# First layer of a two-layer attention kernel: y turned by VectorE and moved through DRAM, statistics moved to ScalarE, each block move one load

## The chip, the cores and the metric

One core of one Trainium2 chip runs the whole kernel in one launch. The metric is the device time of an execution in microseconds, from the first to the last instruction with what lies around it.

## The reference

Two attention layers run over x of shape (32, 256, 256): 32 samples of 256 tokens and 256 features, 16 heads of 16. All is float32.

```python
# layer 0
xn  = layer_norm(x, norm_w, norm_b)
q, k = (xn @ q_w + q_b), (xn @ k_w + k_b)                 # 16 heads
att = softmax(einsum('bnhl,bmhl->bnmh', q, k) + mask, axis=2)
v   = (xn @ v_w + v_b) * src_mask[:, :, None]
y   = einsum('bnmh,bmhl->bnhl', att, v)
h   = layer_norm(y, sb_norm_w, sb_norm_b) * (1 + scale) + shift   # scale, shift from the condition
x   = x + silu(h) @ out_w + out_b
# layer 1: k = softmax over tokens (masked), q = softmax over features, y = q (k^T v), then the same ending
```

## The kernel before, in words

**Stages.** The first layer's attention is a loop of 32 turns `t`, one new sample per turn, in which every engine runs a hand-written order; the tail after it finishes the last samples. Then comes the second layer, as rounds `second(t)`, one sample a round. Semaphores tie the engines together; nothing is scheduled by a tool, so the order of the work is the order of the calls in each engine's block.

**One turn of the first layer.** TensorE computes q, k and v of sample t (`qk`, `vals`), the scores of sample t-1 for their row maxima (`rowmax`, 8 units), the scores again with the maxima subtracted for the exponentials (`scores`, 8 units), and P·V of sample t-4 (`values`, four groups of heads, into the PSUM bank psY, a 17th row giving the sum for the softmax). VectorE reduces the maxima (L1158), ScalarE takes the exponentials (L741) and adds the q and k biases (L764), GpSimd splits q and k into a high and a low part (`split`, L518 and L521), and SyncE issues all DMAs: `parts(t, 0)` and `parts(t, 1)` move six pieces of 256 KB into the tiles Qs and Ks (L326, L328), with a zero block (L323) and mask rows (L320); `c_in` writes the maxima (L346).

**The way of y before.** ScalarE copies psY to the tile yT (`yturn`, L778), TensorE turns it by 128x128 transposes back into psY (L1746), VectorE divides by the sums (`divide`, L1191 and L1193) and takes mean and variance of the rows (`ystats`, L1199 and L1201), GpSimd normalizes (`ynorm`, L503 to L511) into Yn, `ystore` writes Yn to DRAM (L350) and the second half of the kernel loads it by blocks (`yload`, L372, four DMAs).

**The way of x before.** VectorE takes the statistics of x (`stats`, L1090 and L1092), GpSimd normalizes into xs (`xnorm`, L472 to L488), `nstore` writes it to DRAM (L332), `nblocks` loads it back as blocks of 32 rows (L342, four DMAs of 64 KB), and VectorE turns the blocks (`xturn`, L1172). xB, the tile they are loaded into, has one buffer. In the second layer `fstore` and `fload` (L381, L390) do the same for its y. A store before is one DMA with 2 KB in a row, and a load is four DMAs of 512 B runs:

```python
sp.dma_start(xnd[n], xs[:, :, :, :, :].rearrange("p a i k c -> p (a i k c)")).then_inc(s_nd, 16)
...
by_block = xnd[n].rearrange("(b s) (a e) -> a s b e", s=32, a=4)
for q in range(4):
    sp.dma_start(tile[32 * q:32 * q + 32, :, :], by_block[q]).then_inc(s_nb, 16)
```

## Time and profile before

| what | value |
|---|---|
| three runs, median (lowest to highest) | 868.77 us (867.59 to 869.85) |
| the profiled execution | 869.6 us |
| its span, first to last instruction | 867.8 us |
| TensorE busy in the span | 832.3 us (96%) |
| VectorE busy | 773.2 us (89%) |
| ScalarE busy | 679.0 us (78%) |
| GpSimd busy | 679.9 us (78%) |
| mean granted TensorE clock | 0.994 of full speed |
| bytes moved by DMA | 143.69 MB in 129847 packets |

The busy times are of one profiled execution, and are averages over stages that differ: the ramp up to about 80 us, some 26 like turns of the first layer up to about 480 us, its tail up to about 540 us, and the rounds of the second layer. The profile also gives, for any stretch of time, how many packets the core's 16 DMA engines moved and their mean busy share.

### The profile page before, as it was taken

The page shows a single profiled execution, that of the slowest core. Times are in us where ns is not written, and L with a number is a line of the kernel's source. Part 1 is how long each engine was busy: PE and PEld are TensorE (multiplying, and loading weights), DVE is VectorE, ACT ScalarE, POOL GpSimd, SP SyncE. Part 2 cuts the span into 40 slices and gives each one's busy share as a digit, 9 for nine tenths or more (in the row PEclk, how much of TensorE's full clock was granted, in tenths as well). Part 3 has the DMA queues.
Part 4 walks back from the last instruction along what each step waited for, and adds up shares of the span by engine and source line. Part 5 has one row for each costly group of instructions (what it writes and reads, how often), then busy time and mean ns, then how long its engine had stood idle before and what let it go on. Part 6 is the DMA issues. An engine that isn't in the chain of part 4 may idle for free.

```text
span 867.8 us, 23658 instructions
## 1 busy us (share of the span) xinstructions
PE 832.3 (96%) x8092; PEld 686.9 (79%) x8092; DVE 773.2 (89%) x1590; ACT 679.0 (78%) x1208; POOL 679.9 (78%) x1165
## 2 busy tenths in 40 slices
PE   4999999999999999999999988999999999999996
PEld 4777777777777777777777656899999999999996
DVE  6689999999998999999998967899999999999976
ACT  2247777777777777777778796899999999999975
POOL 3375878878888888888786337899999999999965
PEclk9899999999999999999999999999999999999999
DMA  8854665565656565655654424345454444444311
GB/s 258 263 175 165 198 219 187 207 209 191 220 183 212 179 222 181 221 196 196 219 178 164 142 64 107 96 126 144 152 149 143 136 142 140 138 150 141 116 31 62
DMA packets 129847, 143.69 MB, mean 166 GB/s; under 512 B 13312, under 2 KB 85984, under 8 KB 129600
## 3 DMA queue, kind: packets, MB, share of 16 engines
q1 hardware_dynamic: 129728, 142.19, 50.5%
q8 instruction: 65, 1.06, 0.5%
q14 instruction: 54, 0.44, 0.2%
HBM read 49.50 MB, written 38.11 MB: 101 GB/s over the span
## 4 chain that ended last, share of the span: by engine, by line
PE 77%; DVE 13%; issue 6%; POOL 1%; ACT 1%; SPq 1%; DMA 0%; DVEq 0%; ACTq 0%; POOLq 0%
PE psY L1721 12%; PE psX L1600 11%; PE psT L1600 10%; PE psM L1600 10%; DVE sb_cm L1158 6%; PE psT L1700 5%; PE psY L1600 5%; PE psT L1679 4%; PE psT L1883 3%; PE psY L1836 3%; PE psT L1611 3%; PE psM L1700 3%; PE psY L1746 2%; DVE sb_xF L1172 2%; PE psM L1679 2%
## 5 line engine op out<-in xcount | busy, mean ns | idle before, releaser
L1158 DVE TENSOR_REDUCE sb_cm<-psT 128x4 f32<-128x1024 f32 x168 | 202.8, 1213 | 20.5 <-PE psT L1700 20.3
L741 ACT ACTIVATE sb_P<-psT 128x1024 f32<-128x1024 f32 x176 | 177.8, 1026 | 42.6 <-PE psY L1721 23.5
L1721 PE MATMUL psY<-sb_P,sb_Vp 128*17 128x256 f32 x2048 | 129.4, 381 | 1.9 <-DVE sb_yr L1193 1.2
L1158 DVE TENSOR_REDUCE sb_cm<-psM 128x4 f32<-128x1024 f32 x88 | 106.7, 1213 | 11.5 <-PE psM L1700 11.5
L741 ACT ACTIVATE sb_P<-psM 128x1024 f32<-128x1024 f32 x80 | 82.0, 1025 | 21.6 <-PE psY L1721 11.7
L1600 PE MATMUL psX<-sb_xT,sb_W0h 128*128 128x256 f32 x488 | 93.6, 294 | 0.0
L1721 PEld LDWEIGHTS psY<-sb_P,sb_Vp 128*17 128x17 f32 x2048 | 50.3, 97 | 46.8 <-DVE sb_yr L1193 1.9
L521 POOL TENSOR_TENSOR sb_qp<-sb_qp 128x512 fp32r<-128x512 f32 x64 | 82.3, 1285 | 5.3
L1700 PE MATMUL psT<-sb_Ks,sb_Qs 64*128 64x256 f32 x672 | 76.6, 310 | 2.6 <-DVE sb_cm L1158 2.5
L1679 PE MATMUL psT<-sb_Qs,sb_Ks 64*128 64x256 f32 x704 | 75.5, 298 | 1.6 <-ACT sb_P L741 1.4
L1600 PEld LDWEIGHTS psX<-sb_xT,sb_W0h 128*128 128x128 f32 x488 | 71.4, 192 | 4.6 <-ACT sb_qp L764 0.2
L1700 PEld LDWEIGHTS psT<-sb_Ks,sb_Qs 64*128 64x128 f32 x672 | 50.1, 185 | 27.9 <-issue 12.6
L1679 PEld LDWEIGHTS psT<-sb_Qs,sb_Ks 64*128 64x128 f32 x704 | 53.2, 185 | 17.3 <-issue 10.2
L764 ACT ACTIVATE sb_qp<-psX,sb_bq 128x256 f32<-128x256 f32 x122 | 51.1, 472 | 11.0 <-PE psX L1600 11.0
L1600 PE MATMUL psX<-sb_xT,sb_W0l 128*128 128x256 f32 x244 | 48.9, 282 | 0.0
L595 POOL TENSOR_TENSOR sb_rs<-sb_ve,sb_ph 128x2 f32<-128x2 f32 x63 | 44.6, 708 | 5.3
L1746 PE MATMUL psY<-sb_ident,sb_yT 128*128 128x128 f32 x256 | 40.3, 280 | 5.7 <-DVE sb_yr L1193 1.3
L503 POOL TENSOR_SCALAR sb_ve<-sb_mv 128x2 f32<-128x2 f32 x32 | 7.3, 228 | 43.9 <-DVE sb_mv L1201 43.7
L1700 PE MATMUL psM<-sb_Ks,sb_Qs 64*128 64x256 f32 x352 | 40.7, 309 | 0.6 <-ACT sb_P L741 0.5
L1600 PE MATMUL psM<-sb_Woh,sb_v 128*128 128x256 f32 x256 | 41.0, 282 | 0.0
L611 POOL TENSOR_TENSOR sb_v<-sb_v,sb_rb 128x512 f32<-128x512 f32 x32 | 41.0, 1282 | 0.0
L518 POOL TENSOR_SCALAR sb_qp<-sb_qp 128x512 fp32r<-128x512 f32 x64 | 39.7, 621 | 0.7 <-ACT sb_qp L764 0.7
(215 smaller groups left out, 2553.4 us busy)
## 6 DMA issues: line engine op xcount, KB each, us to landing
sb_Qs<-sb_qp SPq DMA_DIRECT2D x96, 256.0 KB
sb_Ks<-sb_qp SPq DMA_DIRECT2D x96, 256.0 KB
sb_xt<-in_x SPq DMA_DIRECT2D x32, 256.0 KB, 3.4
y_normed<-sb_Yn SPq DMA_DIRECT2D x32, 256.0 KB, 2.7
sb_u<-y_normed SPq DMA_DIRECT2D x128, 64.0 KB, 2.6
out<-sb_v SPq DMA_DIRECT2D x31, 256.0 KB, 2.4
x_biased<-sb_xo SPq DMA_DIRECT2D x28, 256.0 KB, 2.3
sb_u<-x_biased SPq DMA_DIRECT2D x28, 256.0 KB, 3.3
```

The costliest lines, as they stand in the source:

```text
L518: g.tensor_scalar(qp[w][:, 0, :, :].bitcast(F32R), qp[w][:, 1, :, :], 1.0, 0.0, ALU.mult, ALU.add)\
L521: g.tensor_tensor(qp[w][:, 1, :, :].bitcast(F32R), qp[w][:, 1, :, :], qp[w][:, 0, :, :], ALU.subtract)\
L595: g.tensor_tensor(rs[:, k], ve[:, k], ph[:, :], ALU.pow).then_inc(e_rs[l], 1)
L611: g.tensor_tensor(x1[n % 7], x1[n % 7], ob1, ALU.add).then_inc(e_xo, 1)
L741: a.activation(P[G % 4][:, :], pairs[place["S", n, g][0]][:, :], ACT.Exp).then_inc(s_ex, 1)
L764: ins = a.activation(qp[w][:, 1, o, :], home("qk"[w], n)[:, T * o:T * o + T], ACT.Identity, bias=bq[:, 2 * w + o:2 * w + o + 1])
L1158: v.tensor_reduce(cm[n % 2][:, 4 * j:4 * j + 4], scores, AX.X, ALU.max, negate=True).then_inc(s_mx, 1)
L1600: ins = pe.matmul(dst, part(lhs[a], d, o), part(rhs[b], d, r), start=(m == 0), stop=(m == 5))
L1679: ins = pe.matmul(pair[:, c:c + 256], Ks[n % RING][p:p + 64, g, 128 * m:128 * m + 128].bitcast(F32R), Qs[n % RING][p:p + 64, g, :].bitcast ...
L1700: ins = pe.matmul(pair[:, c:c + 256], Qs[n % RING][p:p + 64, j, 128 * k:128 * k + 128].bitcast(F32R), Ks[n % RING][p:p + 64, j, :].bitcast ...
L1721: ins = pe.matmul(psY[32 * j:32 * j + 17, y0:y0 + T], Vp[n % RING][:, m, 4 * gr + j, :], Pj[:, c0:c0 + 256], start=(m == 0), stop=(m == 1))
L1746: ins = pe.transpose(psY[:, 128 * q:128 * q + 128], yT[n % 2][:, q, 128 * k:128 * k + 128], ident[:, :])
```

## The change

What it does, part by part:

- **y.** TensorE no longer turns y of samples 0 to 27 (`TAIL = B - 4`), and ScalarE no longer copies it. VectorE turns psY in 32x32 blocks straight into the tile yG (`yblock`), takes the reciprocals (`yroot`), GpSimd multiplies (`share`) into yq, SyncE writes yq to DRAM (`qstore`, runs of 256 B) and loads it back with tokens on the partitions (`qload`), and a turn later VectorE takes the statistics (`ylanded`) and GpSimd normalizes (`ynorm`). Samples 28 to 31 go the old way.
- **x.** From sample 10 on (`SUMMED`) ScalarE makes the sums (`xsum`, `xsquares`, four passes with an accumulator), and GpSimd turns them into mean and variance.
- **masks.** `vmask` moves from GpSimd to ScalarE.
- **block moves.** `nstore`, `ystore` and `fstore` now write 512 B runs in the order the load wants, and `nblocks`, `yload` and `fload` are one DMA each with 2 KB runs.
- **order.** `xturn` on VectorE moves from the middle to the end of a turn; SyncE's `nstore` and `nblocks`, `xstore` and `xload` move ahead of `parts`; the maxima's turn `cturn` moves behind the seventh unit of scores. The heads of a psY group are 4 apart now, and the host packs q's and k's weights accordingly.

```diff
             def nstore(n):
-                sp.dma_start(xnd[n], xs[:, :, :, :, :].rearrange("p a i k c -> p (a i k c)")).then_inc(s_nd, 16)
+                sp.dma_start(xnd[n].rearrange("(s a) (b e) -> b (s a) e", a=4, b=4),
+                             xs[:, :, :, :, :].rearrange("p a i k c -> p a (i k c)")).then_inc(s_nd, 16)
             def nblocks(n):
                 sp.wait_ge(s_nd, 16 * (n - BY_BLOCK + 1))
                 if n > BY_BLOCK:
                     sp.wait_ge(s_xf, n - BY_BLOCK)
-                for q in range(4):
-                    sp.dma_start(tile[32 * q:32 * q + 32, :, :], by_block[q]).then_inc(s_nb, 16)
+                sp.dma_start(xB[:, :, :].rearrange("p k t -> p (k t)"),
+                             xnd[n].rearrange("(s a) e -> a s e", a=4)).then_inc(s_nb, 16)
...
+            def qstore(n):
+                sp.wait_ge(s_yq, 2 * n + 2)
+                sp.dma_start(qd[n].rearrange("r (k j e) -> j (r k) e", k=2, j=4), yq.rearrange("p (x e) -> p x e", e=64))\
+                    .then_inc(s_qd, 16)
+            def qload(n):
+                sp.wait_ge(s_qd, 16 * (n + 1))
+                if n >= 2:
+                    sp.wait_ge(s_y, n - 1)
+                sp.dma_start(yrs[n % 2].rearrange("p k d -> p (k d)"), qd[n].rearrange("(s b) e -> b s e", b=4))\
+                    .then_inc(s_yl[n % 2], 16)
...
+                if 0 <= t - 5 < TAIL:
+                    qstore(t - 5)
+                if t >= BY_BLOCK and ok(t + 2):
+                    nstore(t + 2)
+                if 0 <= t - 5 < TAIL:
+                    qload(t - 5)
+                if 0 <= t - 6 < TAIL:
+                    ystore(t - 6)
...
+                if t >= BY_BLOCK and ok(t + 2):
+                    nblocks(t + 2)
+                    xstore(t + 2)
+                if t >= BY_BLOCK and ok(t + 4):
+                    xload(t + 4)
...
+            def share(n, half):
+                g.wait_ge(s_yi, 2 * n + half + 1)
+                if half == 0 and n >= 1:
+                    g.wait_ge(s_qd, 16 * n)
+                root = ri[:, half, :].rearrange("p (g b a) -> p g b a", g=2, a=1).to_broadcast([128, 2, 8, DH])
+                g.tensor_tensor(yq.rearrange("p (b g d) -> p g b d", b=8, g=4)[:, 2 * half:2 * half + 2],
+                                yG[half][:, :, :, 0:DH], root, ALU.mult).then_inc(s_yq, 1)
...
+            def xsum(n):
+                for k in range(2):
+                    a.activation(xn[:, k, :], xt[n % 2][:, k, :], ACT.Identity, accum_out=sx[:, 0, k:k + 1])\
+                        .then_inc(s_sx, 1)
+            def xsquares(n):
+                for k in range(2):
+                    a.activation(xn[:, k, :], xt[n % 2][:, k, :], ACT.Square, bias=nm[:, k:k + 1],
+                                 accum_out=sx[:, 1, k:k + 1]).then_inc(s_sq, 1)
...
+            def yblock(n, half):
+                v.wait_ge(s_pv, 4 * n + 2 * half + 2)
+                if n >= 1:
+                    v.wait_ge(s_yq, 2 * n - 1 + half)
+                v.transpose(yG[half].rearrange("p g (b k) c -> p g k b c", k=2),
+                            psY[:, :].rearrange("p (g k b c) -> p g k b c", g=2, k=2, c=32)).then_inc(s_yg, 1)
+            def ylanded(n, k):
+                v.wait_ge(s_yl[n % 2], landed(n, 2))
...
-                if ok(t - 4):
-                    yturn(t - 4, 0)
                 rowmax(t, 7)
                 scores(t, 6)
+                if ok(t - 2):
+                    cturn(t - 2)
                 scores(t, 7)
-                if t >= BY_BLOCK:
-                    yturn(t - 4, 1)
                 vals(t)
```

**What moves on SyncE.** One turn of the first layer before, from the store of the normalized x to the first block load (y_normed's store and x's own moves follow it; the numbers behind a tile are the sizes of the written side, slowest first):

```order
L332 DMA x_normed<-sb_xs 128x512 [waits s_xn]
L323 DMA sb_Qs<-sb_zero 4x16x128 [waits s_sT]
L326 DMA sb_Qs<-sb_qp 32x4x512 [waits s_hi]
L326 DMA sb_Qs<-sb_qp 32x4x512
L328 DMA sb_Qs<-sb_qp 32x4x512 [waits s_lo]
L346 DMA sb_Qs<-sb_ct 4x16x128 [waits s_cs]
L320 DMA sb_Ks<-mask_parts 2x8x256 [waits s_sT]
L320 DMA sb_Ks<-mask_parts 2x8x256
L326 DMA sb_Ks<-sb_qp 32x4x512 [waits s_hi]
L326 DMA sb_Ks<-sb_qp 32x4x512
L328 DMA sb_Ks<-sb_qp 32x4x512 [waits s_lo]
L342 DMA sb_xB<-x_normed 32x4x128 [waits s_xf,s_nd]
```

The same place in the changed kernel (qstore, nstore, qload, ystore, nblocks, xstore, xload, then parts):

```order
L368 DMA y_by_block<-sb_yT 4x256x64 [waits s_yq]
L346 DMA x_normed<-sb_xs 4x128x128 [waits s_xn]
L376 DMA sb_yr<-y_by_block 128x1x512 [waits s_y,s_qd]
L363 DMA y_normed<-sb_Yn 4x128x128 [waits s_y]
L354 DMA sb_xB<-x_normed 128x1x512 [waits s_xf,s_nd]
L390 DMA x_biased<-sb_xo 128x512 [waits s_xb]
L289 DMA sb_xt<-in_x 128x2x256
L337 DMA sb_Qs<-sb_zero 4x16x128 [waits s_sT]
L340 DMA sb_Qs<-sb_qp 32x4x512 [waits s_hi]
L340 DMA sb_Qs<-sb_qp 32x4x512
L342 DMA sb_Qs<-sb_qp 32x4x512 [waits s_lo]
L359 DMA sb_Qs<-sb_ct 4x16x128 [waits s_cs]
```

The stores of normalized x and y go from 128x512 to 4x128x128, the store of unnormalized y is 4x256x64, and the block load, which waits for VectorE's xturn (s_xf), stands ahead of the ten DMAs of `parts` and `c_in` instead of behind them. The read side of the three loads is 4x32x512.

**What moves on VectorE.** The middle of a turn before (cm is a reduce of maxima, xF is xturn):

```order
L1158 TENSOR_REDUCE sb_cm<-psT 128x4 [waits s_cx,s_sm]
L1172 STREAM_TRANSPOSE sb_xF<-sb_xB 128x4x4x32 [waits s_xl,s_nb]
L1158 TENSOR_REDUCE sb_cm<-psM 128x4 [waits s_sm]
L1191 RECIPROCAL sb_rd<-psY 128x16 [waits s_y,s_yt]
L1193 TENSOR_TENSOR sb_yr<-psY,sb_rd 128x256 [waits s_yd]
L1158 TENSOR_REDUCE sb_cm<-psT 128x4 [waits s_sm]
L1199 BN_STATS sb_st<-sb_yr 128x6 [waits s_yd]
L1201 BN_AGGR sb_mv<-sb_st 128x2 [waits s_yd]
```

The same place in the changed kernel, up to the end of the turn:

```order
L1289 STREAM_TRANSPOSE sb_yT<-psY 128x2x2x4x32 [waits s_yq,s_pv]
L1256 TENSOR_REDUCE sb_cm<-psT 128x4 [waits s_cx,s_sm]
L1256 TENSOR_REDUCE sb_cm<-psT 128x4 [waits s_sm]
L1294 RECIPROCAL sb_ri<-sb_yT 128x16 [waits s_yg]
L1256 TENSOR_REDUCE sb_cm<-psT 128x4 [waits s_sm]
L1270 STREAM_TRANSPOSE sb_xF<-sb_xB 128x4x4x32 [waits s_xl,s_nb]
L1281 TENSOR_TENSOR sb_vb<-psX,sb_rb 128x512 [waits s_v,s_vm]
```

The division and the wait for TensorE's turn (s_yt) are gone, the transpose of psY stands in their place, and xturn is behind the last reduce of the turn.

## Rows read from the trace of the kernel before

**Rows 1.** The page: span, and busy time, share and instructions of each engine.

```profile
span 867.8 us, 23658 instructions
PE 832.3 (96%) x8092; PEld 686.9 (79%) x8092; DVE 773.2 (89%) x1590; ACT 679.0 (78%) x1208; POOL 679.9 (78%) x1165
```

**Rows 2.** Stretches: length, busy PE PEld DVE ACT POOL, clock, DMA share, GB/s.

```profile
200.00:240.00 40.00, 39.75 (x473) 29.56 (x466) 36.57 (x60) 31.38 (x46) 33.60 (x57) 1.00 0.61 208
...
640.00:680.00 40.00, 40.00 (x300) 38.03 (x299) 38.59 (x104) 37.92 (x84) 36.51 (x64) 1.00 0.47 140
```

**Rows 3.** The chain that ended last, two rounds of the second layer: start, length, work.

```profile
567.55 1.44 PE psY L1600 x12
...
577.74 1.44 PE psY L1600 x12
```

**Rows 4.** Timeline of TensorE, end of a first-layer turn: start, length, instruction.

```profile
314.62 0.60 PE L1746 MATMUL psY<-sb_ident,sb_yT 128*128 128x128 f32 x4
315.15 0.50 PE L1700 MATMUL psT<-sb_Ks,sb_Qs 64*128 64x256 f32 x4
...
316.33 0.66 PE L1746 MATMUL psY<-sb_ident,sb_yT 128*128 128x128 f32 x4
316.74 0.48 PE L1600 MATMUL psX<-sb_W0l,sb_xT 128*128 128x256 f32 x2
```

**Rows 5.** Timeline of VectorE, the same turn and the one before.

```profile
300.63 0.24 DVE L1191 RECIPROCAL sb_rd<-psY 128x16 f32<-128x16 f32 x1
...
313.84 0.70 DVE L1172 STREAM_TRANSPOSE sb_xF<-sb_xB 128x512 f32<-128x512 f32 x1
...
315.57 0.24 DVE L1191 RECIPROCAL sb_rd<-psY 128x16 f32<-128x16 f32 x1
315.85 0.42 DVE L1193 TENSOR_TENSOR sb_yr<-psY,sb_rd 128x256 f32<-128x256 f32 x1
```

**Rows 6.** Groups by line and shape, 201.0 to 395.35 us: ScalarE and GpSimd.

```profile
L778 ACT ACTIVATE sb_yT<-psY 128x512 f32<-128x512 f32 x26 | 15.5, 597 | 0.0
...
L541 POOL TENSOR_SCALAR sb_Vp<-sb_vb,sb_mT 128x256 f32<-128x256 f32 x26 | 12.1, 477 | 0.0
...
L585 POOL TENSOR_TENSOR sb_Wol<-sb_Wo,sb_Woh 128x256 fp32r<-128x256 f32 x2 | 1.5, 740 | 0.0
```

**Rows 7.** Timeline of ScalarE in the second layer: a pass with an accumulator.

```profile
705.95 0.50 ACT L837 ACTIVATE sb_v<-sb_v,sb_kb 128x256 f32<-128x256 f32 x1
```

**Rows 8.** The page: packets of the whole run, and issues with their counts and landings.

```profile
DMA packets 129847, 143.69 MB, mean 166 GB/s; under 512 B 13312, under 2 KB 85984, under 8 KB 129600
...
y_second<-sb_w SPq DMA_DIRECT2D x27, 256.0 KB, 2.0
```

**Rows 9.** Issues of the whole run, the DMAs whose slowest size is small.

```profile
sb_Qs<-sb_zero SPq DMA_DIRECT2D x32, 32.0 KB
sb_Ks<-mask_parts SPq DMA_DIRECT2D x64, 16.0 KB
sb_Qs<-sb_ct SPq DMA_DIRECT2D x32, 32.0 KB
```

**Rows 10.** DMA engines, 318.05 to 318.5 us: packets, then the share of 16 engines.

```profile
DMA packets 65, 0.03 MB, mean 68 GB/s; under 512 B 5, under 2 KB 65, under 8 KB 65
...
q1 hardware_dynamic: 65, 0.03, 24.4%
```

**Rows 11.** DMA engines, 317.0 to 317.9 us, the same two rows.

```profile
DMA packets 119, 0.24 MB, mean 271 GB/s; under 512 B 0, under 2 KB 0, under 8 KB 119
...
q1 hardware_dynamic: 119, 0.24, 71.5%
```

**Rows 12.** Timeline of SyncE: issues of one turn.

```profile
316.80 0.59 SPq L323 DMA_DIRECT2D sb_Qs<-sb_zero  x1
...
322.31 0.60 SPq L328 DMA_DIRECT2D sb_Ks<-sb_qp  x1
...
326.59 0.43 SPq L275 DMA_DIRECT2D sb_xt<-in_x  x1
```

More of the change, by code:

```diff
@@ L49 @@
 BLOCKS = B - 5
+TAIL = B - 4
+SUMMED = BY_BLOCK + 4
 def ok(n):
@@ L144, in bass_cond_seq_kernel @@
         xT1 = [xT[:, :, :], xT2[:, :, :]]
+        blocked, moved = (t[:, :, :].rearrange("p q t -> p (q t)") for t in yT)
+        yG = [blocked[:, 512 * i:512 * i + 512].rearrange("p (g b c) -> p g b c", g=2, b=8) for i in range(2)]
+        yq = moved[:, 0:512]
+        yrs = [yr[:, :, :], moved[:, 512:1024].rearrange("p (k d) -> p k d", k=2)]
         ph = sb("ph", [128, 2])
@@ L236, in bass_cond_seq_kernel @@
             sem(f"s_{n}") for n in ("sT", "ex", "pv", "ye", "yt", "yd", "yr", "y"))
+        s_yg, s_yi, s_yq, s_qd, s_ys = (sem(f"s_{n}") for n in ("yg", "yi", "yq", "qd", "ys"))
+        s_sx, s_sq = sem("s_sx"), sem("s_sq")
+        s_yl = [sem(f"s_yl{i}") for i in range(2)]
         s_yo = [sem(f"s_yo{i}") for i in range(2)]
@@ L386, in fload @@
                     sp.wait_ge(e_u1, n - 1)
[L387 to L390 removed]
+                sp.dma_start(y1T[n % 2].rearrange("p b i k s -> p (b i k s)"),
+                             fd[n].rearrange("(s a) e -> a s e", a=4)).then_inc(e_fl[n % 2], 16)
             def second(t):
@@ L424, in _ @@
                     xload(t + 3)
-                if ok(t + 2) and t + 2 > BY_BLOCK:
+                if t + 1 == BY_BLOCK:
                     nstore(t + 2)
@@ L436, in _ @@
                     nstore(t + 2)
-                if ok(t + 2) and t + 2 >= BY_BLOCK:
+                if BY_BLOCK - 2 <= t < BY_BLOCK:
                     nblocks(t + 2)
+                if t + 1 == BY_BLOCK:
+                    xstore(t + 2)
+                    xload(t + 4)
                 if t + 1 < RING:
@@ L661, in _ @@
                     xlow(t)
-                if BIASED <= t + 1 < B:
-                    xbias(t + 1)
-                for_later(t)
-                if ok(t - 5):
-                    ynorm(t - 5)
+                if ok(t - 5):
+                    share(t - 5, 1)
+                if t >= BY_BLOCK and ok(t + 2):
+                    xnorm(t + 2)
+                if BIASED <= t + 1 <= BY_BLOCK:
+                    xbias(t + 1)
+                if ok(t - 6):
+                    ynorm(t - 6)
+                if ok(t - 4):
+                    share(t - 4, 0)
+                if SUMMED <= t + 3 < B:
+                    xmean(t + 3)
                 if ok(t - 2):
                     csplit(t - 2)
-                if ok(t - 1):
-                    vmask(t - 1)
                 if t + 1 < BY_BLOCK:
                     xnorm(t + 1)
+                elif t + 1 == BY_BLOCK:
+                    xnorm(t + 2)
                 elif ok(t + 2):
-                    xnorm(t + 2)
+                    xbias(t + 2)
+                for_later(t)
                 if ok(t):
@@ L677, in _ @@
                     split(t, 1)
+                if t + 1 == BY_BLOCK:
+                    xbias(t + 2)
                 if t + 2 == BY_BLOCK:
                     xnorm(t + 2)
+            share(B - 5, 1)
+            csplit(B - 2)
+            ynorm(B - 6)
             ynorm(B - 5)
-            csplit(B - 2)
-            vmask(B - 1)
             csplit(B - 1)
@@ L782, in u_ @@
                 if l == 1 and n < BLOCKS:
-                    a.wait_ge(e_fl[n % 2], landed(n, 2, 4))
+                    a.wait_ge(e_fl[n % 2], landed(n, 2))
                 else:
@@ L1203, in yt_ @@
             def yt_(n):
-                v.wait_ge(e_y0[n % 3], landed(n, 3, 4))
+                v.wait_ge(e_y0[n % 3], landed(n, 3))
                 if n >= 2:
```

251 lines of the change are left out of this document (140 added, 111 removed).

## The prediction

> **What bounds the kernel now.** The page comes first: TensorE is busy for 96% of the span, no other engine for more than 89% [rows 1]. That is an average, so the stretches come next. In the first layer's steady turns TensorE is busy 39.75 of 40 us, VectorE 36.57, at full clock, with the 16 DMA engines at 0.61; in the second layer TensorE has 40.00 of 40 and the DMA engines 0.47 [rows 2]. So both long stages go at TensorE's pace, and a mean DMA share looks harmless. VectorE's timeline gives the length of a turn: its first reciprocal comes at 300.63 and again at 315.57, 14.94 us apart (14.95 over thirteen turns) [rows 5]. The chain of waits gives the second layer's round, 10.19 us [rows 3]. The last view is the one this change asks for: short stretches of the DMA engines, because a mean over 16 engines does not tell how many of them a single DMA uses.
>
> **How many engines a DMA uses.** The zero block is written as 4x16x128, 64 runs of 512 B. Just when its packets move, 65 packets keep the engines 24.4% busy over 0.45 us [rows 10]: 3.9 of 16 engines. A piece of q, which begins with 32, has 119 packets of 2 KB in its window of 0.9 us and keeps the engines 71.5% busy, though it runs in the last two thirds of it only [rows 11]: all 16. A count of the whole run says the same. Each DMA ends with one tiny packet on every engine that it used. The list of issues holds 928 DMAs, 32 zero blocks, 32 maxima and 64 masks (2x8x256) among them [rows 9]. With 4 engines for the first two kinds, 2 for the masks and 16 for the other 800 this makes 128 + 128 + 128 + 12800, and with 128 packets of a 144 B load 13312, exactly the packets under 512 B [rows 8]; with 16 everywhere it would be 14976. So a side whose slowest size is 4 puts the whole DMA on 4 engines, here with the narrow side written and a 64 on the other.
>
> The Trainium skill states the rule (DMA: Bandwidth & Descriptors, the section on why a DMA increments its semaphore by 16): the slowest dimension of each side is looked at, and the largest number up to 16 that divides both is taken; on this queue always the lowest-numbered engines. The count above agrees with it. By that rule the loads too, 4x32x512 on the side they read, get 4.
>
> **The change part by part.** Prices of one packet on one engine: 2 KB 0.715 x 16 x 0.9 / 119 = 86.5 ns [rows 11]; 512 B (0.244 x 16 x 0.45 - 5 tiny ones of some 8 ns) / 60 = 28.6 ns [rows 10]; 1 KB on the line between them, about 47.
>
> *DMA engines 0 to 3, first layer, one turn.* All of the new DMAs begin with 4 on one side, and I take the same four engines for all (the narrow DMAs of before did not show otherwise). Store of normalized x: 512 runs over 4 engines, 128 x 28.6 = 3.66 us. Store of normalized y: 3.66. Block load of x and load of y: 32 packets x 86.5 ns = 2.77 each. The new store of y has 1024 runs of 256 B, 256 per engine. The trace has no such packet: by bytes at the 512 B rate 14.3 ns, by packets 28.6; I take 20, a little under the middle, since the fixed share seen in tiny packets is small: 5.1 us, with 3.7 and 7.3 as bounds. Unchanged and spread over 16: six pieces of q and k, 48 packets, 4.15; x biased 0.69; x itself 16 x 47 = 0.75. Zero and maxima 0.92, masks 0.75 on two of the four. Sum 3.66 + 3.66 + 2.77 + 2.77 + 5.1 + 4.15 + 0.69 + 0.75 + 0.92 + 0.75 = 25.2 us, against a turn of 14.95. Before, the same engines had 4.15 + 0.69 x 2 + 0.75 + 1.67 and the blocks evenly spread, some 9.
>
> Do these four engines stay busy? SyncE issues `qstore` and `nstore` right behind `parts`, and `ystore` before it waits for `xturn`; while it waits for a landing another transfer is queued each time. VectorE's xturn follows the landed K by about 5 us, while the two stores, the load and y's store still take 15. So the queue does not run dry, and the turn is 25.2 us. GpSimd's `share`, which waits for the store of the sample before (s_qd), and SyncE behind it, then wait inside this period, not on top of it.
>
> *Sum, first layer.* Turns 6 to 29 have all of it: 24 x (25.2 - 14.95) = +246. Turns 30 and 31 lack x: 25.2 - 3.66 - 2.77 - 0.69 - 0.75 = 17.3, +5. Turns 28 and 29 lack `xload`, -1.5; turns 4 and 5 and the later landing of y in the tail +4. Together +253.
>
> *Second layer, one round, the same four engines.* yload 2.77, fstore 3.66, fload 2.77, x 0.69, key mask 8 x 47 = 0.38, output 0.75: 11.0 us. `fload` waits for the landing of `fstore`, and nothing else is queued then: a landing took 2.0 us for 0.7 us of transfer [rows 8], so a gap of 1.3. A round of 12.3 against 10.2: 26 x 2.1 = +55.
>
> *The compute engines, hidden under this.* TensorE loses two groups of four transposes a turn, 0.53 and 0.41 us from start to start [rows 4], and a short wait for VectorE before one: -1.1. VectorE loses two reciprocal-and-divide pairs (0.28 + 0.34) and two statistics of x (0.55 each) and gains two transposes of 512 columns, 0.63 each as xturn [rows 5], and two reciprocals: -0.6. ScalarE loses two copies of 0.60 [rows 6] and gains four passes with an accumulator of 0.50 [rows 7] and two mask passes of about 0.45: +1.7 on about 10.7. GpSimd loses two mask passes of 0.48 and gains two multiplies of 0.74 [rows 6]: +0.5 on 12.9. None comes near 25 us; what hides them is the DMA, and without it they would be a turn of about 14.
>
> Sum: 869.6 + 253 + 55 = 1177.6 us by the profiled execution, which lies 0.8 above the median of the runs; I say **1177**.
>
> **Rivals.**
> 1. *Loads spread over 16.* Only the written side may decide; every narrow DMA of the trace was narrow where it wrote. Each load then costs 0.69: a turn is 25.2 - 2 x 2.08 = 21.0, the second layer's sum 6.9 and hidden. 24 x 6.1 + 2 = +148: 1018 us. Chance 0.14.
> 2. *All of it spread over 16, and the kernel is faster.* It decides if a narrow side written to DRAM is treated otherwise than one in on-chip memory; all narrow ones above were written on chip. Then the turn is between TensorE's 14.95 - 1.1 = 13.85 and a new loop: xturn now ends the turn, `nblocks` waits for it, three issues of some 0.45 and the row from the zero block to the last K piece, 322.91 - 316.80 = 6.1 us [rows 12], with about 2 us to land, stand before the next sample's first scores, and xturn again about 5 us later: 14.5. At 14.3 over 26 turns: -17, 853 us; at 13.85 841. Against it: the exact count. Chance 0.08.
> 3. *Runs of 256 B cost far more.* At twice a 512 B packet, 57 ns, the store takes 14.6 us, the turn 34.7, and the time is 1177 + 24 x 9.5 = 1405. Nothing in the trace speaks for it: the tiny packets are the cheapest. Chance 0.06. The Trainium skill has such a rule (DMA: Bandwidth & Descriptors, Specifications): below 512 B the engine reads, modifies and writes. No run here shows it.
> 4. *In between*: the queues overlap better than the sum, or a lower TensorE clock, granted in waits of 10 us, lengthens the loops: 0.04 over both sides of the forecast.
>
> **How the numbers follow.** The forecast has 0.68. Its own bounds are 24 x (3.7 - 5.1) = -34 and 24 x 2.2 = +53 for the 256 B runs: 1143 to 1230; a missing overlap of 1 us or a slow clock adds to the upper one, 1270. The range goes down to rival 1: **1000 to 1270**, leaving out rivals 2 and 3 with 0.14 and a little of the rest. About 0.3% (2.6 us) is what a measurement can tell from no change: faster 0.08, same 0.02, slower 0.90.
>
> **What would show it.** A turn of 25 us between `xturn`s, with the mean DMA share not higher but lower than 0.61 and TensorE busy about 55%; stretches with only `nstore` at 24% of 16 engines, 3.7 us long; `x_normed` stores that take 5 us or more to land instead of 2; packets under 512 B that, less the 256 B ones, count 4 per block move. Waits of TensorE's scores and of `qk` on DMA and GpSimd, not on VectorE. It is wrong if those stores land in 2 to 3 us, or if the turn comes near 14 us; rival 1 shows itself in a block load that lands in 2.5 us.

## The result, and the profile after

The changed kernel takes 1342.03 us (median of four runs, 1341.69 to 1342.89); the kernel before, on the same chip, 868.35 us. The ratio is 1.545, 95% interval 1.543 to 1.548. The forecast was 1177 us with a range of 1000 to 1270: the side is right, the time lies 72 us above the range. The ratios and medians here and below leave disturbed executions out: in e_wide two of its four, 953.1 and 955.2 us, the first of them the one whose profile is read.

The page of the changed kernel: span, busy times, packets, queue, the chain that ended last, and one group of section 5.

```profile
span 1341.1 us, 23227 instructions
...
PE 963.5 (72%) x7868; PEld 766.8 (57%) x7868; DVE 774.1 (58%) x1502; ACT 715.9 (53%) x1392; POOL 667.7 (50%) x1157
...
DMA packets 156205, 158.32 MB, mean 118 GB/s; under 512 B 36088, under 2 KB 108760, under 8 KB 155960
...
q1 hardware_dynamic: 156088, 156.84, 38.7%
...
DMA 54%; SPq 20%; PE 8%; issue 5%; ACT 5%; DVE 4%; POOL 3%; ACTq 0%; DVEq 0%; POOLq 0%
...
L890 ACT ACTIVATE sb_v<-sb_w,sb_FB,sb_FA 128x256 f32<-128x256 f32 x54 | 29.5, 592 | 166.7 <-DMA sb_w<-y_second 166.7
```

No compute engine is near full now, where TensorE had 96% [rows 1], and over half of the chain is DMA, though the DMA queue takes only 38.7% of 16 engines' time. The small packets say where that comes from. The page counts 36088 under 512 B. Besides the 1024 runs of 256 B of each of 28 stores, 28672, these are 7416 tiny ones. The page lists 226 block moves (28 + 28 of y_by_block, 26 + 26 of x_normed, 32 + 32 of y_normed, 27 + 27 of y_second) and 375 other DMAs on 16 engines (the 800 of before less its 425 block moves). With 4 tiny packets per block move this makes 904 + 6000 + 128 (zero) + 128 (maxima) + 128 (masks) + the 128 of the 144 B load [rows 8, 9] = 7416, exactly. So **every block move, load or store, uses 4 engines**.

The same two stretches as before (first layer, second layer), with the same columns as [rows 2]:

```profile
200.00:240.00 40.00, 25.47 (x269) 17.83 (x269) 21.37 (x34) 19.98 (x40) 22.85 (x37) 0.88 0.52 159
1040.00:1080.00 40.00, 30.46 (x172) 28.69 (x173) 23.08 (x58) 24.25 (x54) 20.44 (x37) 0.76 0.26 77
```

In the second layer the mean DMA share is 0.26 while TensorE sits idle a quarter of the time at a granted clock of 0.76. That 0.26 is near 4 of 16 by chance, and does not mean four engines always busy: by the packet records of the same trace no packet at all is under way in 18% of the time from 1040 to 1178 us. The second layer waits on something else than the four engines' throughput.

Where the 473.3 us between the two spans lie is read from two instructions: xturn on VectorE, once a turn, and fstore on SyncE, once a round. First and last start, in the timelines by line of the kernel after and then of the kernel before:

```profile
L1270 DVE STREAM_TRANSPOSE sb_xF<-sb_xB x26: 700/702/711, 93.5 to 718.5; 128x512 f32<-128x512 f32 x26
...
L406 SPq DMA_DIRECT2D y_second<-sb_w x27: 551/558/559, 834.6 to 1282.0; - x27
```

```profile
L1172 DVE STREAM_TRANSPOSE sb_xF<-sb_xB x26: 700/702/703, 89.5 to 463.3; 128x512 f32<-128x512 f32 x26
...
L381 SPq DMA_DIRECT2D y_second<-sb_w x27: 327/338/338, 551.9 to 816.5; - x27
```

| stretch | before | after | difference |
|---|---|---|---|
| up to the first xturn | 89.5 | 93.5 | +4.0 |
| 25 turns of the first layer | 373.8 (14.95 each) | 625.0 (25.0 each) | +251.2 |
| last xturn to first fstore | 88.6 | 116.1 | +27.5 |
| 26 rounds of the second layer | 264.6 (10.18 each) | 447.4 (17.2 each) | +182.8 |
| from the last fstore on | 51.3 | 59.1 | +7.8 |

The first layer came as forecast (25.2 a turn); the second did not (12.3 a round forecast, 17.2 measured). One round of it in the chain of waits (start, length, what):

```profile
1005.52 1.09 ACT sb_v L916 x2
1006.61 0.02 issue
1006.63 0.72 DVE sb_w L1338
1007.36 0.02 issue
1007.37 6.67 DMA y_second<-sb_w
1014.04 0.02 issue
1014.06 6.58 DMA sb_w<-y_second
1020.64 0.03 issue
...
1022.33 0.58 ACT sb_v L960
1022.90 0.99 ACT sb_v L916 x2
1023.89 0.02 issue
1023.91 0.72 DVE sb_w L1338
1024.63 0.02 issue
1024.65 6.67 DMA y_second<-sb_w
```

The chain closes on itself: store, 6.7 us; load, 6.6; ScalarE's `u_` (L890), which waits for that load; behind it in ScalarE's order `yn_` (L916) of the next sample; VectorE turns that (L1338); and this is what the next store takes. Both narrow landings and some 4 us of compute stand in series: 17.3 us. (`u_` reads a sample's y after its store and load, `yn_` prepares the y of the next sample for its store.)

For the first layer, the DMA engines in ten pieces of one turn (columns as above; the last three are clock, DMA share, GB/s):

```profile
400.00:402.50 2.50, 2.50 (x46) 1.36 (x44) 2.50 (x3) 1.41 (x4) 2.42 (x3) 1.00 0.27 93
402.50:405.00 2.50, 1.58 (x20) 1.31 (x17) 2.35 (x5) 2.04 (x4) 2.50 (x3) 1.00 0.34 106
405.00:407.50 2.50, 2.50 (x34) 1.89 (x33) 1.39 (x4) 0.00 (x0) 2.14 (x6) 1.00 0.86 275
407.50:410.00 2.50, 0.34 (x8) 0.00 (x0) 0.79 (x2) 0.00 (x0) 2.09 (x5) 1.00 0.84 252
410.00:412.50 2.50, 0.00 (x0) 0.00 (x0) 0.00 (x0) 1.19 (x5) 0.00 (x0) 0.82 0.58 213
412.50:415.00 2.50, 1.28 (x8) 0.99 (x8) 0.98 (x1) 2.38 (x4) 0.00 (x0) 0.50 0.62 219
415.00:417.50 2.50, 2.50 (x24) 0.93 (x24) 0.53 (x2) 1.02 (x1) 0.00 (x0) 0.50 0.30 79
417.50:420.00 2.50, 2.50 (x24) 2.36 (x22) 2.50 (x3) 1.02 (x1) 0.00 (x0) 0.82 0.28 62
420.00:422.50 2.50, 1.66 (x17) 1.07 (x15) 2.19 (x4) 2.02 (x4) 2.00 (x5) 1.00 0.24 52
422.50:425.00 2.50, 2.50 (x30) 2.23 (x32) 0.92 (x3) 2.45 (x7) 2.42 (x4) 1.00 0.26 81
```

The share is 0.24 in its lowest piece: four engines' worth is busy in every piece, and in six of the ten there is hardly more. That is the picture of a queue that does not run dry. The packet records of the trace say it more finely: from 200 to 450 us there are at least four packets under way in 92% of the time and never none, where the kernel before has at least four in 67% (200 to 349 us) and none in 18%. They do not name the engine of a packet.

And the price of a 256 B run, in a window in which the new store of y moves almost alone:

```profile
DMA packets 549, 0.15 MB, mean 74 GB/s; under 512 B 545, under 2 KB 545, under 8 KB 549
...
q1 hardware_dynamic: 549, 0.15, 31.7%
```

That is 416 to 418 us: 0.317 x 16 x 2 us, less the four 2 KB packets, over 545 packets: each is under way for 18 ns. But 0.317 x 16 is 5.1 engines' worth on four engines, so the packets' times overlap. Counted by throughput, 545 packets over four engines in 2 us, a run takes 14.7 ns of an engine, where the forecast took 20.

### The profile page after: what moved, and what is told of

Read it like the earlier page. It is cut to its first block, busy times and chain, and to the rows that moved or that the text cites. A ratio compares the mean times of both kernels' runs of the same rounds, so it can differ in the third digit from the quotient of the medians.

```text
span 1341.1 us, 23227 instructions
## 1 busy us (share of the span) xinstructions
PE 963.5 (72%) x7868; PEld 766.8 (57%) x7868; DVE 774.1 (58%) x1502; ACT 715.9 (53%) x1392; POOL 667.7 (50%) x1157
## 2 busy tenths in 40 slices
DMA packets 156205, 158.32 MB, mean 118 GB/s; under 512 B 36088, under 2 KB 108760, under 8 KB 155960
## 3 DMA queue, kind: packets, MB, share of 16 engines
q1 hardware_dynamic: 156088, 156.84, 38.7%
## 4 chain that ended last, share of the span: by engine, by line
DMA 54%; SPq 20%; PE 8%; issue 5%; ACT 5%; DVE 4%; POOL 3%; ACTq 0%; DVEq 0%; POOLq 0%
DMA x_normed<-sb_xs 22%; DMA y_second<-sb_w 14%; DMA sb_w<-y_second 13%; SPq L340 5%; DMA y_by_block<-sb_yT 5%; SPq L354 4%; SPq L342 3%; SPq L334 2%; ACT sb_v L916 2%; PE psX L1729 1%; DVE sb_w L1338 1%; SPq L337 1%; ACT sb_v L890 1%; SPq L359 1%; SPq L390 1%
## 5 line engine op out<-in xcount | busy, mean ns | idle before, releaser
L554 POOL TENSOR_TENSOR sb_yT<-sb_yT,sb_ri 128x256 f32<-128x256 f32 x56 | 34.8, 622 | 307.2 <-DMA y_by_block<-sb_yT 178.1
L1829 PE MATMUL psT<-sb_Ks,sb_Qs 64*128 64x256 f32 x672 | 90.9, 359 | 95.8 <-ACT sb_P L804 89.2
L1849 PE MATMUL psY<-sb_P,sb_Vp 128*17 128x256 f32 x2048 | 152.5, 433 | 8.3 <-DVE sb_yr L1311 7.8
L1957 PE MATMUL psY<-sb_v 128*128 128x128 f32 x256 | 61.9, 418 | 127.9 <-ACT sb_v L960 125.4
L1957 PEld LDWEIGHTS psY<-sb_v 128*128 128x128 f32 x256 | 53.6, 309 | 140.2 <-ACT sb_v L960 137.2
L890 ACT ACTIVATE sb_v<-sb_w,sb_FB,sb_FA 128x256 f32<-128x256 f32 x54 | 29.5, 592 | 166.7 <-DMA sb_w<-y_second 166.7
L1729 PE MATMUL psX<-sb_xT,sb_W0h 128*128 128x256 f32 x488 | 100.4, 310 | 14.6 <-POOL sb_xT L546 14.5
L1808 PE MATMUL psT<-sb_Qs,sb_Ks 64*128 64x256 f32 x704 | 89.0, 336 | 19.6 <-DMA sb_Qs<-sb_ct 18.7
L845 ACT ACTIVATE sb_xn<-sb_xt 128x256 f32<-128x256 f32 x44 | 17.9, 408 | 156.8 <-DMA sb_xt<-in_x 156.8
L804 ACT ACTIVATE sb_P<-psM 128x1024 f32<-128x1024 f32 x80 | 81.5, 1018 | 36.4 <-PE psM L1808 27.0
L1729 PEld LDWEIGHTS psX<-sb_xT,sb_W0h 128*128 128x128 f32 x488 | 76.4, 205 | 26.2 <-POOL sb_xT L546 19.1
L1289 DVE STREAM_TRANSPOSE sb_yT<-psY 128x512 f32<-128x512 f32 x56 | 39.7, 710 | 59.8 <-PE psY L1849 59.7
L1829 PEld LDWEIGHTS psM<-sb_Ks,sb_Qs 64*128 64x128 f32 x352 | 31.6, 219 | 61.9 <-ACT sb_P L804 47.0
```

The costliest lines, as they stand in the source:

```text
L804: a.activation(P[G % 4][:, :], pairs[place["S", n, g][0]][:, :], ACT.Exp).then_inc(s_ex, 1)
L890: ins = a.activation(dst, blocks, ACT.Identity, bias=FB[:, l, d, n:n + 1], scale=FA[:, l, d, n:n + 1])
L1729: ins = pe.matmul(dst, part(lhs[a], d, o), part(rhs[b], d, r), start=(m == 0), stop=(m == 5))
L1808: ins = pe.matmul(pair[:, c:c + 256], Ks[n % RING][p:p + 64, g, 128 * m:128 * m + 128].bitcast(F32R), Qs[n % RING][p:p + 64, g, :].bitcast ...
L1829: ins = pe.matmul(pair[:, c:c + 256], Qs[n % RING][p:p + 64, j, 128 * k:128 * k + 128].bitcast(F32R), Ks[n % RING][p:p + 64, j, :].bitcast ...
L1849: ins = pe.matmul(psY[32 * j:32 * j + 17, y0:y0 + T], Vp[n % RING][:, m, 4 * j + gr, :], Pj[:, c0:c0 + 256], start=(m == 0), stop=(m == 1))
```

## The experiments

Two questions: is the second layer's loss that loop and nothing else, and is the first layer's turn the four engines' sum, or a chain of waits that happens to be as long? In all kernels but b_f_narrow and b_12_issues the edit is to the changed kernel. Turn and round are read from xturn and fstore as above.

| run | median us | ratio, interval | turn | round |
|---|---|---|---|---|
| after | 1342.0 | 1.545, 1.543 to 1.548 | 25.0 | 17.2 |
| e_f_old | 1155.1 | 1.332, 1.327 to 1.336 | 25.0 | 10.35 |
| b_f_narrow | 1053.3 | 1.213, 1.209 to 1.218 | 14.96 | 17.1 |
| e_narrow_mid | 1338.8 | 1.543, 1.539 to 1.547 | 25.1 | 17.1 |
| e_narrow_two | 1337.6 | 1.538, 1.531 to 1.546 | 24.9 | 17.2 |
| e_x_old | 1266.9 | 1.458, 1.451 to 1.465 | 22.3 | 17.1 |
| e_loads_wide | 1176.6 | 1.358, 1.352 to 1.364 | 22.2 | 14.2 |
| e_all_old_moves | 988.1 | 1.138, 1.134 to 1.142 | 19.1 | 10.2 |
| e_wide | 944.3 | 1.088, 1.078 to 1.098 | 18.1 | 10.2 |
| e_q5 | 957.0 | 1.104, 1.099 to 1.109 | 18.1 | 10.4 |
| e_q5_two | 950.4 | 1.091, 1.085 to 1.098 | 17.8 | 10.3 |
| e_q5_xb2 | 897.3 | 1.032, 1.029 to 1.035 | 16.2 | 10.3 |
| e_q5_last | 904.6 | 1.042, 1.038 to 1.045 | 16.0 | 10.3 |
| b_12_issues | 916.7 | 1.056, 1.053 to 1.060 | 16.8 | 10.2 |
| e_reorder | 1432.0 | 1.648, 1.643 to 1.654 | 28.8 | 17.1 |
| e_wide_reorder | 1141.2 | 1.314, 1.307 to 1.322 | 25.2 | 10.3 |
| e_q5_reorder | 1146.9 | 1.320, 1.314 to 1.327 | 25.4 | 10.2 |
| e_q5_mid | 996.8 | 1.149, 1.145 to 1.153 | 19.9 | 10.3 |
| e_q5_mid_two | 995.2 | 1.145, 1.138 to 1.152 | 19.7 | 10.3 |

### The second layer

**e_f_old.** `fstore` and `fload` as before, all else changed:

```diff
-                sp.dma_start(fd[n].rearrange("(s a) (b e) -> b (s a) e", a=4, b=4), y1s).then_inc(e_fd, 16)
+                sp.dma_start(fd[n], y1s.rearrange("p a e -> p (a e)")).then_inc(e_fd, 16)
...
-                sp.dma_start(y1T[n % 2].rearrange("p b i k s -> p (b i k s)"),
-                             fd[n].rearrange("(s a) e -> a s e", a=4)).then_inc(e_fl[n % 2], 16)
+                for q in range(4):
+                    sp.dma_start(tile[32 * q:32 * q + 32, :, :], by_block[q]).then_inc(e_fl[n % 2], 16)
```

> The changed kernel with only the second layer's move of y (fstore and fload) as before: one store of 128 rows of 2 KB and four loads of 32x4x128. Theory (the round of 17.3 us is a loop: the store's landing of 6.7 us, the load's landing of 6.6 us and some 4 us of ScalarE and VectorE, in series, because ScalarE waits in order in u_ for the load and the next sample's yn stands behind it): with both moves wide the two landings shrink to some 2 us each, the loop is shorter than TensorE's 10.2 us, and the round returns to 10.2: 27 x 7.1 = 192 us less, 1150 us, with a first-layer turn still of 25.0 us. Rival (the four engines' sum per round sets the round, 11.0 + 1.3 as forecast, and the remaining 5 us come from something else in the round, such as the lower clock): taking 6.4 us of transfer off the sum leaves a round of 12 us or more, 1200 us. Second rival (the load of y_normed, still narrow, holds the round): round 11 to 12.

1155.1 us, a round of 10.35, the turn unchanged. The two moves carry 187 us. The load of y_normed, still on four engines, does not hold the round.

**b_f_narrow.** The mirror: the kernel before with these two moves narrow.

> The kernel before with one part of the change alone: fstore and fload as the change has them, on four engines. Theory (the loop through the two landings, with nothing of the rest of the change): first layer as before, the round 17.2 instead of 10.2 us, 868 + 26 x 7.0 = 1050 us. Rival (the round of 17.2 needs the narrow load of y_normed too, which shares the four engines): a round of 14 to 15 us, 970 to 990 us. Forecast as it was (sum of the engines, here 7.8 us and hidden): no change.

1053.3 us, a round of 17.1. Its chain of waits:

```profile
699.78 1.09 ACT sb_v L819 x2
...
700.89 0.72 DVE sb_w L1215
701.61 0.02 issue
701.63 6.23 DMA y_second<-sb_w
707.86 0.02 issue
707.87 7.00 DMA sb_w<-y_second
```

The same loop at the same length with nothing of the rest of the change. By the forecast's rule for the second layer this kernel would hardly have slowed. With y_normed's load spread over 16 engines the four carry 11.0 - 2.77 + 0.92 = 9.2 us (the expectation's 7.8 leaves out the key mask and the output), and with the forecast's gap of 1.3 a round is 10.5 us, some 8 us in all. It slowed by 184 us.

### The first layer, narrow

SyncE's timeline in the changed kernel shows 12.8 us a turn in which it stands before a full queue and two landings, so "SyncE in its order" was a rival for the 25.0 us. The first attempt at it moved two things, and one of them spoiled it:

**e_reorder.** `nstore` ahead of `qstore`, `qload` behind the last piece of k.

> The changed kernel, all its narrow DMAs kept, with SyncE's order changed alone: nstore ahead of qstore, and qload behind the last piece of k instead of right behind its store. So SyncE no longer stands still for the landing of y_by_block, and x_normed is not queued behind its 1024 runs. Two theories of the first layer's turn of 25.0 us. Sum (as forecast: the four engines have 25.2 us of packets a turn): the order changes nothing, a turn of 25 us, 1342 us. SyncE (its time in order is the turn: some 11.5 us of issues and 12.8 us in which it stands before a full queue or a landing): the wait falls from 12.8 to some 7 us, a turn of 19 to 20 us, 1342 - 25 x 5.5 = 1205 us, and the four engines never had 25 us of work.

1432 us: slower than either theory allows. VectorE takes the statistics of y in order, ahead of its maxima, and now waited for the late load (240 to 480 us; total, times, longest):

```profile
DVE sb_st L1301 <- DMA sb_yr<-y_by_block: 50.3, 4, 13.0
DVE sb_st L1301 <- DMA sb_yT<-y_by_block: 48.7, 4, 12.3
```

The edit had closed a loop of its own (pieces of k, qload, statistics, maxima), and tells nothing on the question.

**e_wide_reorder, e_q5_reorder.** The same order with all moves on 16 engines fell to the same wait; the case is told by e_reorder.

> The kernel with every block move on 16 engines (18.1 us a turn, 952 us) with the same new order on SyncE. SyncE theory: its 26 issues a turn at 0.57 us are 14.9 us, and the waits for the landing of y_by_block and for xturn (some 3 us) go: a turn of 15 to 15.5 us, 952 - 25 x 2.8 = 882 us. Rival (GpSimd's share, which waits for the store of the sample before, or the loop through xturn holds the 18.1 us): no change, 945 to 955 us.

> As the last one, with y_by_block stored by one DMA (2 KB per partition in two runs of 1 KB, all 16 engines; yblock writes its blocks in the order that this wants) and loaded by four of 32x8x64, runs of 256 B. 23 issues a turn, 13.1 us at 0.57. SyncE theory: now TensorE's 13.85 us or the loop of 14.3 us is the turn, 841 to 855 us, a little faster than the kernel before. Rival (SyncE's issues are not the bound): no better than the last one.

**e_narrow_mid** is the clean form: `nstore` ahead of `qstore` again, but `qload` behind `xload`, ahead of the pieces of q.

```diff
-                if 0 <= t - 5 < TAIL:
-                    qstore(t - 5)
                 if t >= BY_BLOCK and ok(t + 2):
                     nstore(t + 2)
                 if 0 <= t - 5 < TAIL:
-                    qload(t - 5)
+                    qstore(t - 5)
...
                     xload(t + 4)
+                if 0 <= t - 5 < TAIL:
+                    qload(t - 5)
```

> The changed kernel with all its narrow DMAs, nstore ahead of qstore and qload behind xload. Decides over the turn of 25.0 us. Sum theory (the four engines' packets): 25 us, 1342 us. SyncE theory (12.8 of the 25.0 us are SyncE before a full queue and two landings in series): one of the landings goes, a turn of 20 to 21 us, 1342 - 25 x 4.5 = 1230 us.

1338.8 us, a turn of 25.1. SyncE's two waits for landings are gone from its list of waits from 240 to 480 us. It stands for xturn (17.3 us) and for GpSimd's x (17.4 us) instead, and the turn did not move.

**e_narrow_two.** A second buffer for yq, `share` waits for the store two samples before.

> The changed kernel, all narrow, with two buffers yq instead of one, so that GpSimd's share of a sample waits for the store of y_by_block two samples before, not one. Share theory (share waits in order for that landing, and cturn's operand and the split of q and k stand behind it on GpSimd; this closes a loop of 25 us): the loop opens, a turn of 21 us or less, 1240 us. Sum theory (the four engines have 25.2 us of packets a turn, GpSimd waits inside it): no change, 1335 to 1345 us.

1337.6 us, a turn of 24.9. Three orders and bufferings, one turn: the sum theory holds, and it alone said so beforehand. One rival is left: two loops of equal length, of which each run opened only one, or the loop through xturn and its single buffer, which no narrow kernel opened. Against it stand the packet records: in these two kernels as well at least four packets are under way in 90 to 92% of the time (200 to 450 us) and never none, so there was little left to gain by opening a loop.

**e_x_old, e_loads_wide.** Traffic taken off the four engines: the moves of x_normed as before, or all loads split into four DMAs of 32x512.

```diff
-                sp.dma_start(xB[:, :, :].rearrange("p k t -> p (k t)"),
-                             xnd[n].rearrange("(s a) e -> a s e", a=4)).then_inc(s_nb, 16)
+                for q in range(4):
+                    sp.dma_start(tile[32 * q:32 * q + 32, :], by_block[q]).then_inc(s_nb, 16)
```

> The changed kernel with only the moves of x_normed as before (one store of 128 rows, four loads of 32x4x128). Sum theory: the four engines lose 3.66 + 2.77 and gain 0.69 + 0.92: 25.0 - 4.8 = 20.2 us a turn, 1342 - 25 x 4.8 = 1222 us, second layer still 17.2 a round. Rival (landings of x_normed in SyncE's order set the 25 us): they shrink to 3 us, the turn to 18 us as with all moves wide, 1167 us.

> The changed kernel with its new stores (narrow, on four engines) and its four loads each split into four DMAs of 32x512, on 16 engines. Theory: a turn is the sum 25.0 - 2 x 2.77 + 2 x 0.69 = 20.8 us; a round of the second layer loses 4.4 us of the load's landing, 12.9 us; 1342 - 26 x 4.2 - 27 x 4.4 = 1114 us. Rival (loads and stores do not cost alike: the store's landing and its 1024 small packets are what holds, the loads are hidden behind them): little changes in the first layer, 24 us a turn, and 1342 - 26 - 119 = 1197 us.

1266.9 and 1176.6 us, turns of 22.3 and 22.2 where the sum gives 20.2 and 20.8. The round of e_loads_wide is 14.2 us where 12.9 was expected, 3.0 us less and not 4.4: in its chain of waits the last of the four loads lands in 2.2 us, as expected, but the issues of the three before it, 1.3 us with the gaps, now stand in the chain too. Taking 4.8 and 4.2 us off shortened the turn by 2.7 and 2.8 only, so something else, between 20 and 22 us, lies close below. In e_x_old the lowest of the ten pieces from 400 to 425 us has a DMA share of 0.15, and by its packet records fewer than four packets are under way in 21% of the time from 200 to 423 us, none at all in 5%: there the four engines do run dry. That the next bound is the loop shown below for the wide kernel, with narrow landings in it, is likely and wasn't tested.

### The first layer, wide

**e_all_old_moves, e_wide.** The moves of x_normed, y_normed and y_second as before; e_wide has y_by_block stored by four DMAs of 32x4x2x64 and loaded by four of 32x512 too, so that every block move is on 16 engines.

```diff
+                for j in range(4):
+                    sp.dma_start(by_group[j], yq.rearrange("p (q k e) -> p q k e", k=2, e=64)[32 * j:32 * j + 32])\
+                        .then_inc(s_qd, 16)
...
+                for b in range(4):
+                    sp.dma_start(yrs[n % 2].rearrange("p k d -> p (k d)")[32 * b:32 * b + 32, :], by_token[b])\
+                        .then_inc(s_yl[n % 2], 16)
```

> The changed kernel with the moves of x_normed, y_normed and y_second all as before; only the new way of y through y_by_block (qstore, qload) stays on four engines. Theory (the turn is the sum of what the four engines carry): 25.0 - 3.66 x 2 - 2.77 + 0.69 x 2 + 0.92 = 17.2 us a turn, second layer 10.2 a round: 870 + 24 x 2.3 + 5 = 930 us. Rival (the turn is made of landings in SyncE's order, x_normed's above all, and not of the sum): with x_normed wide the turn falls to the compute engines' 14 to 14.5 us, 855 to 865 us.

> The changed kernel with every block move on all 16 engines: those of before for x_normed, y_normed and y_second, and y_by_block stored by four DMAs of 32x4x2x64 and loaded by four of 32x512. This is the rest of the change without its narrow DMAs. Theory (the narrow DMAs carry the whole loss): a turn between TensorE's 13.85 us and the loop of 14.3 us (xturn at the turn's end, store, load, q and k pieces, scores), so 841 to 853 us, clock back at full speed. Rival (part of the loss is in the other parts: ScalarE's statistics, the order of xturn, the issues of SyncE, now 8 more a turn): a turn of 15 us or more, 870 to 900 us.

988.1 and 944.3 us, where 930 and 841 to 853 were expected, with turns of 19.1 (17.2 expected) and 18.1. Of the 474 us some 400 go with the narrow moves, and some 75 stay: the rest of the change is slower too, a turn of 18.1 us and not 14.3. Three causes were tried.

**e_q5.** SyncE's issues: y_by_block stored by one DMA, 23 issues a turn for 26. yblock writes its blocks in another order to make this possible, and y_by_block is loaded in runs of 256 B.

```diff
+                sp.dma_start(qd[n].rearrange("r e -> (r e)").rearrange("(k p f) -> p k f", k=2, p=128),
+                             yq.rearrange("p (k f) -> p k f", k=2)).then_inc(s_qd, 16)
```

> Every block move on 16 engines in the changed kernel's own order, y_by_block stored by one DMA instead of four: 23 issues a turn instead of 26. SyncE theory (its 26 issues at 0.57 us, 15 us, and two waits of 1.5 us make the turn of 18.1 us): three issues fewer are 1.7 us less a turn, 16.4 us, 952 - 25 x 1.7 = 909 us. Rival (a loop that does not run through SyncE's issues, as GpSimd's wait for the store before it writes yq again): no change, 945 to 955 us.

957.0 us, no gain, and the same turn of 18.1. From 240 to 440 us SyncE stands 25.5 us for xturn where e_wide has 11.2, and 21.8 for the store of y_by_block where e_wide has 11.4; that store, now one DMA, lands in 3.1 us and not 2.2. So the time of the saved issues went into waits, and the number of issues alone does not bound the turn. **e_q5_mid** (qload behind xload) made it worse, as VectorE then waits for y's load, up to 4.0 us a time:

> As e_q5, with qload moved from right behind nstore to behind xload, ahead of the first piece of q: SyncE no longer stands for the landing of y_by_block, and VectorE's statistics of y a turn later still find it in time (in the order that put it behind the last piece of k VectorE waited 9 us for it each turn). SyncE theory: 1.5 us less a turn than e_q5, 15 us, 870 to 880 us. Rival: nothing, as for e_q5.

**e_q5_two, e_q5_mid_two.** GpSimd's wait: two buffers yq.

> Every block move on 16 engines, y_by_block stored by one DMA (957 us, 18.1 us a turn), with the two buffers yq. Share theory (the loop q and k pieces, qstore's issue, its landing of 4.4 us, share, csplit, cturn, c_in sets the 18.1 us): the loop opens and the turn falls to 15 or 15.5 us, SyncE's 23 issues and its two waits, 957 - 25 x 2.8 = 885 us. Rival (still something else): 945 to 960 us.

> As e_q5_two, with qload behind xload, so that SyncE does not stand for the landing either. With one buffer this order gave 997 us against 957, VectorE then waiting 3 us a turn for the load. With two the landing comes earlier only if share does: 885 us if SyncE's wait is what remains, 920 or more if VectorE's wait for the load, in order ahead of the maxima, is a loop of its own.

950.4 and 995.2 us, 7 us or less for the second buffer in either order: this wait is not it either. But the trace of e_q5_two shows the loop. SyncE and VectorE, in parts of one turn (timelines, start, length):

```profile
304.65 0.70 DVE L1277 STREAM_TRANSPOSE sb_xF<-sb_xB 128x512 f32<-128x512 f32 x1
...
323.20 0.70 DVE L1277 STREAM_TRANSPOSE sb_xF<-sb_xB 128x512 f32<-128x512 f32 x1
```

```profile
305.43 1.73 SPq L357 DMA_DIRECT2D sb_xB<-x_normed  x4
...
308.15 0.59 SPq L338 DMA_DIRECT2D sb_Qs<-sb_zero  x1
...
314.48 0.60 SPq L343 DMA_DIRECT2D sb_Ks<-sb_qp  x1
...
323.98 1.73 SPq L357 DMA_DIRECT2D sb_xB<-x_normed  x4
```

`nblocks` waits for xturn, because xB has one buffer; the pieces of q and k stand behind it on SyncE; and the next xturn, at the end of VectorE's turn, stands behind the maxima that need them. From the end of xturn to the end of the issue of the last piece of k 9.7 us, then 8.1 us to the next xturn and 0.7 for it: 18.5 here, 17.8 in the mean.

**e_q5_xb2.** Two buffers for xB:

```diff
-                if n > BY_BLOCK:
-                    sp.wait_ge(s_xf, n - BY_BLOCK)
+                if n > BY_BLOCK + 1:
+                    sp.wait_ge(s_xf, n - BY_BLOCK - 1)
```

> Every block move on 16 engines, two buffers yq (950 us, 17.8 us a turn), and two buffers for xB, so that nblocks waits for xturn of the turn before last and SyncE no longer stands for xturn ahead of the pieces of q and k. Xturn loop (rival 2 of the forecast, taken there at 14.5 us; by this trace 305.37 to 315.12 us from xturn's end to the issues of nblocks, x and the six pieces, 9.7, then 3.5 to land and 5 to the next xturn, 18.2): the loop opens and the turn falls to SyncE's own 23 issues and its wait of 1.9 us for y_by_block, 15 us; 950 - 25 x 2.8 = 880 us. Rival (no such loop, or the next one stands just behind): 935 to 955 us.

897.3 us, a turn of 16.2 (15 was expected): 53 us go with that one wait, so the loop is shown. Now SyncE's list of waits (240 to 440 us) begins with the landing of y_by_block:

```profile
SPq L380 <- DMA y_by_block<-sb_yq: 11.2, 6, 3.0
SPq L380 <- DMA y_by_block<-sb_yT: 10.7, 6, 2.1
```

**e_q5_last.** qload behind nblocks, against that wait.

> The wide kernel with two buffers yq and two xB (897 us, 15 to 16 us a turn), with qload moved from right behind nstore to behind nblocks, ahead of xstore. In the kernel without this move SyncE's turn is 13.1 us of issues and 1.9 us before the landing of y_by_block. If that is the bound now, the turn falls to TensorE's 14 us, 897 - 24 x 1.5 = 861 us, level with the kernel before or a little faster. Rival (VectorE's statistics of y then wait for the later load, as in the earlier move of qload): 897 us or more.

904.6 us, no gain. SyncE now stands 19.9 us in the same stretch for the landing of x_normed instead: the wait was moved, not removed. The best version of the change stays 3.2% behind the kernel before; what holds its last 28 us is not settled.

**b_12_issues.** What SyncE's issues cost, in the kernel before: twelve more DMAs of 1 KB a turn, into a scratch tensor.

> The kernel before with twelve more DMAs a turn on SyncE in turns 6 to 29, ahead of nstore, each of 1 KB (16 partitions of 64 B into a scratch tensor): bytes and engine time of next to nothing, issues of some 0.45 us. SyncE theory: its turn before is 11 us of issues and a wait of some 4 us; twelve more make 11 + 5.4 = 16.4 to 17 us, above TensorE's 14.95, so 868 + 24 x 1.7 = 905 to 920 us. Rival (issues are hidden beside TensorE as before): 868 us.

916.7 us, a turn of 16.8. The twelve take 5.5 us, 0.46 each, and SyncE hardly waits any more:

```profile
304.73 5.53 SPq L429 DMA_DIRECT2D more<-sb_ident  x12
```

## Why the prediction was wrong, step by step

- **Which engines a DMA uses**: right. 36088 small packets are accounted for one by one with 4 per block move, loads included. Rival 1 (loads on 16, 1018 us) falls with it. The rule of the Trainium skill (DMA: Bandwidth & Descriptors, the section on why a DMA increments its semaphore by 16) agrees for reads and writes.
- **Price of 256 B runs**: 14.7 ns by throughput for the assumed 20, near the forecast's lower bound of 14.3. Rival 3 (57 ns) falls; the rule of the Trainium skill on transfers below 512 B (DMA: Bandwidth & Descriptors, Specifications) did not show as a higher price per packet here.
- **First layer, 25.2 us a turn**: 25.0 measured, and e_narrow_mid and e_narrow_two bear out that it is the sum. "GpSimd's share waits inside this period" holds too: with a second buffer nothing moves. Another bound was closer than the forecast knew: with less traffic the turn falls to 22, not to 20. And the exact number owes something to luck. As an estimate from the prices measured since (34 ns for a 512 B packet standing alone, next point), the two stores of normalized x and y cost 1.4 us more than forecast, and the store of y 1.3 us less; the two errors cancel.
- **"A round of 12.3 against 10.2: 26 x 2.1 = +55"**: this is the step that failed. The sum of the four engines, 11.0, is not what a round waits for. The two landings, 6.7 and 6.6 us, lie in series with ScalarE's `u_` and `yn_` and VectorE's transposition, since ScalarE takes them in order. Measured: 26 x 7.03 = +183, and +8 behind it. The sizes inside were off as well: the store was priced at 3.66 us of transfer, and its landing took 6.67. In b_f_narrow, where the store moves alone, 403 packets keep the engines 24.3% busy over 3.5 us, 34 ns for a 512 B packet and not 28.6. The gap put behind the store (1.3 us) was that of a landing of before, while the chain has two landings of 6.6 us and more. The miss is 190.6 - 55 = 136 us here, and 282.7 - 253 = 30 us in the ramp, the turns and the tail together, most of it in the 27.5 us from the last turn to the first round.
- **The range** took its bounds from the price of one packet and from an overlap missed in the first layer. It had no case in which the second layer's chain closes, though the forecast named the wait of fload for fstore itself. Following ScalarE's order behind that wait once round would have shown it.
- **"None comes near 25 us; without it they would be a turn of about 14", and rival 2 at 853 us**: wrong for the wide kernel, though it played no part in the time. The loop through xturn, nblocks and the pieces was named, and priced at 14.5; in e_q5_two it is 17.8. The forecast's parts were three issues (1.35) + 6.1 + 2 + 5; the trace has 9.7 from xturn's end to the last piece's issue, in which nblocks has four issues (1.7) where the forecast counted one, and 8.1 for the 7, and xturn itself (0.7) was left out.
- **What would show it**: the turn, the small packets, the DMA share below 0.61 (0.52) and the landing of x_normed's store (12.1 us at 413.13, 5 or more forecast) came as said, TensorE's share of a turn a little above the 55% (64%). Not as said: from 200 to 450 us TensorE's longest waits are for ScalarE's exponentials (59.9 us), not for DMA (4.5) or GpSimd (12.3).
